# A four-layer graph stack on one core: layer 0 reads a turned copy of x, the gate's column rows come from v, and the first loads and all lists are set anew

## The reference

```python
# layer 0: 8 heads of 32, masked attention, layer norm
q, k, v = (proj(Wq, bq), proj(Wk, bk), proj(Wv, bv))
scores = jnp.where(mask, q @ k^T / sqrt(32), -inf)
x = layernorm(x + softmax(scores) @ v @ Wo.T + bo) * gamma + beta
# layer 1: 8 heads, gate a + c, log of the adjacency
a = x @ w_g[:D]
c = x @ w_g[D:]
scores = scores + (a[:, :, None] + c[:, None, :] + b_g + log(adjacency + EPS))
x = softmax(scores) @ V + x
# layer 2: graph attention, one head
logits = q + jnp.swapaxes(k, 2, 1); masked = logits + (1 - adj) * NEG_BIG
x = softmax(leaky(masked)) @ feat_proj + x
# layer 3: as layer 0, with log(clip(adj)) added to the scores
```

## Time and profile before

| | |
|---|---|
| median of 3 runs | 1913.1 us (1909.35 to 1915.19) |
| the profiled execution | 1908.63 us, span 1906.8 us |
| PE, DVE busy | 92%, 81% of the span |
| ACT, POOL busy | 64%, 65% of the span |
| transfers | 66.44 MB, 35 GB/s on average |

### The profile page before, as it was taken

How to read it: one execution, slowest core, us unless ns; L and a number is a source line. 1 busy time by engine, 2 the same in 40 slices (tenths; PEclk the granted TensorE clock), 3 DMA queues, 4 the chain that set the end, 5 groups by cost and what they waited for, 6 DMA issues and landing times.

```text
span 1906.8 us, 54647 instructions
## 1 busy us (share of the span) xinstructions
PE 1745.8 (92%) x23564; PEld 1334.6 (70%) x23564; DVE 1550.6 (81%) x2976; ACT 1216.3 (64%) x1894; POOL 1230.1 (65%) x743
## 2 busy tenths in 40 slices
PE   3899998899999999889999989888999999988996
PEld 2667776677777777577777767667777677766774
DVE  2889887777799988777889988777788998877775
ACT  1567665467777775456877767546777776654675
POOL 2534588368874377728895348754888445883688
PEclk9999999999999999999999999999999999999999
DMA  5110000100221001000111000010021100001001
GB/s 138 40 40 18 13 18 29 41 19 29 63 68 35 13 18 35 17 29 24 51 57 62 24 19 13 30 45 7 19 74 57 51 19 13 18 29 40 13 18 46
DMA packets 67731, 66.44 MB, mean 35 GB/s; under 512 B 6050, under 2 KB 67492, under 8 KB 67492
## 3 DMA queue, kind: packets, MB, share of 16 engines
q1 hardware_dynamic: 67492, 62.95, 11.1%
HBM read 54.54 MB, written 8.39 MB: 33 GB/s over the span
## 4 chain that ended last, share of the span: by engine, by line
PE 74%; DVE 19%; ACT 2%; issue 2%; SPq 1%; POOL 1%; DMA 0%; DVEq 0%; POOLq 0%; ACTq 0%
PE gx L589 22%; PE sc L694 16%; PE od L727 16%; PE gx L740 5%; PE gx L614 3%; PE sc L688 3%; DVE ring L969 3%; PE sc L700 3%; PE gx L776 3%; DVE negm L941 2%; DVE negm L944 2%; DVE qk L923 2%; PE gx L707 2%; DVE lg L1013 1%; DVE negm L957 1%
## 5 line engine op out<-in xcount | busy, mean ns | idle before, releaser
L574 POOL TENSOR_TENSOR ring<-ring,adj_c 128x1024 f32<-128x1024 f32 x256 | 610.4, 2409 | 170.0 <-ACT ring L837 113.0
L694 PE MATMUL sc<-qk 32*128 32x256 f32 x9216 | 417.4, 297 | 11.2 <-ACT m_rows L827 4.4
L694 PEld LDWEIGHTS sc<-qk 32*128 32x128 f32 x9216 | 326.0, 187 | 110.1 <-issue 64.3
L824 ACT ACTIVATE aside<-sc 128x1024 f32<-128x1024 f32 x192 | 196.6, 1024 | 236.1 <-PE sc L694 156.3
L941 DVE TENSOR_REDUCE negm<-sc 128x4 f32<-128x1024 f32 x192 | 234.1, 1219 | 86.2 <-PE sc L694 51.8
L839 ACT ACTIVATE ring<-sc 128x1024 f32<-128x1024 f32 x256 | 248.4, 1023 | 29.8 <-PE sc L700 29.3
L727 PE MATMUL od<-ring,vf 128*32 128x256 f32 x3072 | 243.4, 388 | 3.2 <-POOL ring L574 3.2
L553 POOL TENSOR_TENSOR xs<-xs,bo 128x512 f32<-128x512 f32 x96 | 128.0, 1333 | 182.0 <-DVE xt_lo L915 169.4
L727 PE MATMUL od<-ring,ones_r 128*32 128x256 f32 x3072 | 236.1, 379 | 0.0
L944 DVE TENSOR_REDUCE negm<-aside 128x4 f32<-128x1024 f32 x192 | 232.3, 1210 | 0.0
L579 POOL TENSOR_TENSOR xs<-xs,lr_g 128x512 f32<-128x512 f32 x64 | 86.9, 1357 | 169.8 <-ACT xs L846 169.8
(11 more groups left out here) (141 smaller groups left out, 4320.5 us busy)
## 6 DMA issues: line engine op xcount, KB each, us to landing
adj_c<-in_adj_t SPq DMA_DIRECT2D x96, 256.0 KB, 2.8
adj_r<-in_adj SPq DMA_DIRECT2D x64, 256.0 KB, 2.9
xs<-in_x SPq DMA_DIRECT2D x32, 256.0 KB, 3.1
out<-xs SPq DMA_DIRECT2D x32, 256.0 KB, 2.2
wo<-in_w_o SPq DMA_DIRECT2D x2, 256.0 KB
ring<-in_w_q SPq DMA_DIRECT2D x2, 256.0 KB, 6.5
ring<-in_w_k SPq DMA_DIRECT2D x2, 256.0 KB, 6.7
lr_g<-in_w_bg SPq DMA_DIRECT2D x2, 128.0 KB
```

Of the source, the lines that this page charges most:

```text
L574: pool.tensor_tensor(part, part, adj_c[i.mi % 3][:, t, :].unsqueeze(1).to_broadcast([P, G, N]), ALU.mult).then_inc(weighted, 1)
L694: mm = pe.matmul(sc[:, g, t * N:(t + 1) * N], buf[rows, a, c, t * P:(t + 1) * P], buf[rows, b, c, :], start=(n == 0 and not masked), stop= ...
L824: act.activation(aside[:], sc[:, 0:2, :], ACT.Copy).then_inc(set_aside, 1)
```

## The change

- **x of layer 0.** The host passes a turned copy `x_t` as well. A new stage LT on SP loads it into two buffers `x_raw`. In layer 0 T is only ACT's copy to `xt_hi` and DVE's `xt_lo`, both from `x_raw`; the four PE transposes are gone. LT waits until the `xt_lo` of the item two before is done, ACT's T until the projections that read the buffer are.
- **Gate's c.** `cr_hi`, `cr_lo`, `row_sel` and the six matmuls are gone. A new stage O takes column D + 1 of `vf`: two small DVE operations put its hi and lo into `c_pad`, two 128x128 matmuls turn it into `gx`, ACT copies it to `c_rows`.
- **First loads.** x_t of item 0 is SP's first load. ACT issues the weights q, k, v of layer 0 and their two bias columns on its own queue. The operands of `fold_biases` come next, the other small ones (`plain`) and the weights of layers 1 to 3 behind x of item 1. `extend_fc` now also waits for `w_plain`. POOL's scaling of q1 and q3 moves to PC of item 1.
- **Lists.** All tables have new numbers (GAT_START 24 to 25 and LAST_START 33.5 to 37.5 leave the order of the items as it is).

The diff, cut to its core (of the tables only some lines; of the functions the lines spoken of here):

```diff
-    "T": {PE: [-1.369], ACTE: [-0.812], DVE: [-0.531]},
-    "A": {PE: [13.457, 13.547, 15.008, 15.85]},
+    "T": {ACTE: [-1.791], DVE: [-1.732]},
+    "A": {PE: [13.511, 14.151, 14.428, 15.543]},
-    "U": {DVE: [7.002]},
-    "H": {DVE: [19.026]},
+    "O": {PE: [3.901], ACTE: [3.712], DVE: [2.701]},
+    "U": {DVE: [7.447]},
+    "H": {DVE: [18.738]},
+    "LT": {SP: [-10.005]},
...
+            sp.dma_start(x_raw[0][:], x_t_all[items_l0[0].batch]).then_inc(xt_loaded[0], 16)
+            sp.dma_start(adj_r[0][:], adj_all[rows_of[0].batch]).then_inc(adjr_loaded[0], 16)
+            for dst, src in fold_plain:
+                sp.dma_start(dst, src).then_inc(w_fold, 16)
+            sp.dma_start(x_raw[1][:], x_t_all[items_l0[1].batch]).then_inc(xt_loaded[1], 16)
             for s, i, c in order[SP]:
-                if s == "LX":
+                if s == "LT" and i.i0 >= 2:
+                    sp.wait_ge(xt_lo_set, items_l0[i.i0 - 2].k + 1)
+                    sp.dma_start(x_raw[i.i0 % 2][:], x_t_all[i.batch]).then_inc(xt_loaded[i.i0 % 2], 16)
+                elif s == "LX":
                     if i.k == GROUP - 1:
                         sp.wait_ge(w_lo_set, len(WEIGHTS))
                     if i.group:
                         sp.wait_ge(stored[i.slot], 16 * i.group)
                     sp.dma_start(xs[:, i.slot], x_all[i.batch]).then_inc(x_loaded[i.slot], 16)
-                    if i.k == 0:
-                        for dst, src in first_plain:
-                            sp.dma_start(dst, src).then_inc(w_first, 16)
-                        for n in range(3):
+                    if i.k == 1:
+                        for dst, src in plain:
+                            sp.dma_start(dst, src).then_inc(w_plain, 16)
+                        for n in range(3, len(WEIGHTS)):
                             load_weight(n)
                 elif s == "LR":
...
-                        pool.wait_ge(w_plain, 16 * len(plain))
-                    pool.wait_ge(xt_lo_set, i.k + 1)
+                    if i.l == 0:
+                        pool.wait_ge(*x_ready(i))
+                    else:
+                        pool.wait_ge(xt_lo_set, i.k + 1)
...
                 elif s == "PC":
+                    if i.k == 1:
+                        pool.wait_ge(w_plain, 16 * len(plain))
+                        for name in ("q1", "q3"):
+                            pool.tensor_scalar(b_col[name][:], b_col[name][:], SCALE, None, ALU.mult).then_inc(cols_set, 1)
...
-                pe.wait_ge(w_plain, 16 * len(plain))
+                pe.wait_ge(w_fold, 16 * len(fold_plain))
...
-                    if s == "P" and i.l == 1:
-
-                        if newcomer:
-                            pe.wait_ge(cw_set, CW_STEPS)
-                        pe.wait_ge(*gx_emptied("ca", i))
-                        project(gx_of("ca", i)[:, 0:N], [lambda h: cr_hi[:, h, :], lambda h: cr_lo[:, h, :]],
-                                [lambda h: xh[:, h, :], lambda h: xl[:, h, :]]).then_inc(gx_sem("ca", i), 1)
...
+                elif s == "O":
+
+                    pe.wait_ge(c_pad_set, i.i1 + 1)
+                    pe.wait_ge(*gx_emptied("ca", i))
+                    for n in range(T):
+                        mm = pe.matmul(gx_of("ca", i)[:, n * P:(n + 1) * P], c_pad[i.i1 % 2][:, n, :], ident_r[:], start=True, stop=True)
+                    mm.then_inc(gx_sem("ca", i), 1)
...
+            for n in range(3):
+                if n == 1:
+                    for dst, src in first_plain:
+                        act.dma_start(dst, src).then_inc(w_first, 16)
+                name = WEIGHTS[n]
+                act.dma_start(staged[name][:, :, 0:D], w[name].rearrange("(c p) e -> p c e", p=P)).then_inc(w_raw[n], 16)
             split(0)
             for s, i, c in order[ACTE]:
                 newcomer = i.group == 0 and i.slot == 0
                 if s == "I":
                     split(c)
                 elif s == "T":
-                    act.wait_ge(gx_sem("x", i), gx_count("x", i))
-                    act.activation(xt_hi[i.k % 2][:].rearrange("p c n -> p (c n)"), gx_of("x", i)[:], ACT.Copy)\
-                        .then_inc(xt_hi_set, 1)
+                    hi = xt_hi[i.k % 2][:].rearrange("p c n -> p (c n)")
+                    if i.l == 0:
+                        act.wait_ge(xt_loaded[i.i0 % 2], 16 * (i.i0 // 2 + 1))
+                        if i.k >= 2:
+
+                            j = items[i.k - 2]
+                            what = "fp1" if j.l == GAT else "vb" if j.l == 1 else "v"
+                            act.wait_ge(gx_sem(what, j), gx_count(what, j))
+                        act.activation(hi, x_raw[i.i0 % 2][:].rearrange("p c n -> p (c n)"), ACT.Copy).then_inc(xt_hi_set, 1)
+                    else:
+                        act.wait_ge(gx_sem("x", i), gx_count("x", i))
+                        act.activation(hi, gx_of("x", i)[:], ACT.Copy).then_inc(xt_hi_set, 1)
...
-                    if s == "P" and i.l == 1:
-                        act.wait_ge(gx_sem("ca", i), gx_count("ca", i))
-                        act.activation(c_rows[i.i1 % 2][:], gx_of("ca", i)[:, 0:N], ACT.Copy).then_inc(c_hi_set, 1)
...
+                elif s == "O":
+                    act.wait_ge(gx_sem("ca", i), gx_count("ca", i))
+                    act.activation(c_rows[i.i1 % 2][:], gx_of("ca", i)[:, 0:N], ACT.Copy).then_inc(c_set, 1)
...
+                dve.wait_ge(w_plain, 16 * len(plain))
...
-                    dve.tensor_tensor(xt_lo[i.k % 2][:].rearrange("p c n -> p (c n)"), gx_of("x", i)[:],
+                    turned_x = x_raw[i.i0 % 2][:].rearrange("p c n -> p (c n)") if i.l == 0 else gx_of("x", i)[:]
+                    dve.tensor_tensor(xt_lo[i.k % 2][:].rearrange("p c n -> p (c n)"), turned_x,
...
                                                  op0=ALU.add, op1=ALU.subtract).then_inc(qk_lo_set, 1)
-                    if s == "P" and i.l == 1:
-                        dve.wait_ge(c_hi_set, i.i1 + 1)
-                        rows = c_rows[i.i1 % 2]
-                        dve.scalar_tensor_tensor(out=rows[:], in0=rows[:].bitcast(F32), scalar=row_sel[:],
-                                                 in1=gx_of("ca", i)[:, 0:N], op0=ALU.mult, op1=ALU.add).then_inc(c_lo_set, 1)
...
+                elif s == "O":
+                    gate_c = vf[i.mi % NVF][:, :, D + 1:D + 2].to_broadcast([P, T, G])
+                    pad = c_pad[i.i1 % 2][:].rearrange("p t (g r) -> p t g r", g=G)
+                    dve.wait_ge(v_set, v_count(i))
+                    if i.i1 >= 2:
+                        dve.wait_ge(c_set, i.i1 - 1)
+                    dve.tensor_copy(pad[:, :, :, 0], gate_c).then_inc(c_hi_set, 1)
+                    dve.wait_ge(c_hi_set, i.i1 + 1)
+                    dve.tensor_tensor(pad[:, :, :, 1], gate_c, pad[:, :, :, 0].bitcast(F32), ALU.subtract).then_inc(c_pad_set, 1)
```

207 lines of the change are left out of this document (91 added, 116 removed).

## The result

| | time, us |
|---|---|
| before, median of 4 runs | 1911.9 (1909.35 to 1915.19) |
| after, median of 4 runs | 2080.8 (2077.0 to 2083.6) |
| ratio | 1.088, 95% interval 1.085 to 1.091 |
| profiled execution, before and after | spans 1906.8 and 2076.6 |

A forecast was written before the change was run, and what follows sets the result against it. The prediction took TensorE as the bound (busy 1745.8 of 1906.8 us), with PE waiting for others in layer 1. Start, layer 0 and layer 1's lock: 1908.6 - 20 - 4 + 24 + 8 = 1916.6, as a median 1921; range 1862 to 1946.

The forecast's parts named there:

- The start: Before the first Q: Q starts at about 7 us, W_fc's extension at 27; -20 us, bounds -25 and -12.
- rival D: First loads queue up behind each other, so the start gains only 12 us; 1929 us, chance 0.08.
- Layer 0: Its 32 items: removed turning matmuls save 0.53 us each, mostly lost again; -4 us, bounds -16 and +5.
- the gap: Layer 0 on PE: S, now directly behind P, waits for E's exps, 0.44 us plus 0.05 for the semaphore.
- Layer 1, own work: PE in layer 1: six matmuls on c leave, two for O come; -0.5 us an item, bound -16 for 32.
- Layer 1, DVE against POOL: POOL's ring multiply holds up U on DVE: items take 17.9 us instead of 15.3; +24, and +8 for Z items.
- rival C: PE's clock halves after idle stretches, 1.7 us each, four more per group, +27; 1948 us, chance 0.12.
- step (c): Layer 1 on DVE: H comes before U, so U starts 0.60 us later.
- The multiply: Layer 1 on POOL: E.1's ring multiply does not move; XB and PC fit into 3.48 us of POOL idle time.
- the norm's items: Layer 1, fourth and fifth item of a run, with Z: 1 us each for 8 items, +8.
- the first three: First three layer 1 items of each run, mixed with layer 0: 0, from -1.5 to +3 for all three.
- The rest: GAT: 0; layer 3: 0, bound +2.7 an item on the 20 without Z if the lock comes there.

The follow-up runs named there:

- h0: Kernel before with only the new first loads (x of item 0 first, not turned), all tables old: 1897.6 us, ratio 0.989.
- f2: Changed kernel with all its new tables, but stage O removed and c made by six matmuls behind P as before: one run, 2129.5 us.
- f4: Kernel before with one number changed: in layer 1 U stands behind H on DVE; one run, 2013.2 us.
- e2b: Changed kernel's code with the tables of the kernel before, except new layer 1 table and FIRST_PLAN left new: one run, 2099.9 us.
- experiments 1 and 2: Changed kernel's code, tables of the kernel before except FIRST_PLAN and O's own places: 2127.9 us; then the same with the new layer 1 table: 2099.9 us.
- h2: Kernel before with new first loads, U ahead of N on DVE in layer 1, POOL's Y behind E.0's multiply: 1880.8 us, ratio 0.980.
- g4: Changed kernel with POOL's layer 1 order and layer 0's Y (ACT, POOL) as before, U and O ahead of N and H on DVE: one run, 1935.9 us.

## Why the prediction was wrong

**The start: right in size but for its gate.** Q started at 7.0 as said. W_fc's extension started at 31.9 and not at 27, 15 us earlier than before and not 20. h0 gives the same: 25.1 us earlier and 9.3 lost again in layer 0, so some 16 where 20 was forecast with a bound of 12. The chain of waits:

```profile
15.35 10.27 DMA ring<-in_w_q
...
25.64 0.63 ACT wh_q L788
...
31.96 0.57 DVE ring L897
```

What was late was not W_fc but w_q of layer 1: issued at 15.35, it took 10.27 us to land, and its split stands in ACT's list ahead of work that item 1 needs. I had followed DVE's list to its load and not ACT's. The same load took 7.59 us in the kernel before, as SP's 25th; here it is the 30th and takes 10.27. That is what rival D spoke of: the loads did run into each other. That the Trainium skill, page "DMA: Bandwidth & Descriptors", section "Issuing engines are not separate DMA queues", says that such transfers share the same engines agrees with it.

**Layer 0: the gap came, and the bound was too small.** In the first group the first row below shows S's wait for the exps: 0.65, of which 0.23 is one of the four mask matmuls whose record is missing, so some 0.42 (forecast 0.44 and the semaphore). Items took 17.0 and not 17.4, in part since of three A's in a row the first two take 0.87 each, where single ones took 1.0. In the later groups the first three took 19.8 to 21.4 and the others 17.7 to 19.1. Timeline of PE in the first group, then of POOL, DVE and PE in a later one:

```profile
113.12 0.81 PE L681 MATMUL sc<-mask_r,ident_b 128*128 128x512 bf16 x3 [0.65 <-ACT ring L854]
...
603.43 2.15 POOL L581 TENSOR_TENSOR xs<-xs,lr_e 128x512 f32<-128x512 f32 x1
...
602.78 3.88 DVE L980 TENSOR_TENSOR ring<-ring,adj_c 128x1024 f32<-128x1024 f32 x2
...
612.77 1.29 POOL L549 TENSOR_TENSOR xs<-xs,bo 128x512 f32<-128x512 f32 x1
...
612.85 1.76 DVE L922 TENSOR_TENSOR xt_lo<-x_raw,xt_hi 128x512 fp32r<-128x512 f32 x1
...
611.87 0.62 PE L687 MATMUL sc<-qk 32*128 32x256 f32 x12 [1.67 <-DVE negm L943]
```

L980 takes 3.88 for two beside Y, so the reduction behind it on DVE (L943) ends late, and E, which needs the score buffer that it reads, waits 1.67. Behind that, L922 takes 1.76 beside XB. U is held more often in layer 0, too: in layer 0 of group 1 its two operations take 873 and 975 ns on average, where they took 466 and 516, and `xt_lo` 1395 instead of 680. That is 7 us more of DVE for U and 5 for `xt_lo`, in a group that became 13 us longer; which of it PE waited for is not set apart. The prediction had looked at U in layer 1 alone. It said of DVE that it would be full and of L922 that it could be held up, and left both at 0, with +5 for the whole as a bound. It was +47, the start's late gate included. A row of the groups of the kernel before would have given a bound (busy us, mean ns):

```profile
L969 DVE TENSOR_TENSOR ring<-ring,adj_c 128x1024 f32<-128x1024 f32 x128 | 181.6, 1459 | 0.3 <-issue 0.3
```

Half of these rows take no more than 1.22 us; the mean of 1459 says that even before, a sixth of their time was waiting for POOL.

**Layer 1, own work: not measured by itself.** Forecast were -0.5 us an item. f2 shows O worth 1.2 us an item against the six matmuls, but in lists where POOL holds DVE up, so that this holds more than the matmuls.

**Layer 1, DVE against POOL: the mechanism right, the size off by 4.** This is the step that failed. Forecast +32, measured +139, of which PE's idle time is +101 and most of the rest the clock. Three terms of the step were mis-sized:

- *The clock.* I had it as rival C at 1.7 for an idle stretch, one in five already there, and at 0 in the forecast. The step (c) alone costs 3.4 by the clock (f4: 8.76 against 5.32), and in the changed kernel the clock is at half for 10.24 us in each item, behind and through PE's two waits. The earlier trace rows had 0.98 because four of five items hardly idled; the mean hid what one idle stretch costs. It could be read there: the item behind the 2.69 us of idle in the earlier trace rows (Q at 731.50) took 16.8 us with PE busy all through at a clock of 0.90, and the one behind it 15.3 us. Five items a group at 3.4 would have made +68.
- *The multiply.* The prediction said that it does not move. It did. ACT's part of Y stands behind P now, so POOL's Y starts at 285.89, and E.0's multiply behind it ends at 293.2 instead of having ended before O. I had placed XB and PC into an idle time of 3.48 us that Y's delay had used up. So O, which I took to be free, was held for 2.3 us.
- *O on PE's path.* PE waits at O's matmuls between A.2 and A.3 (2.46), for O's operations and for H behind them. I had costed O's operations on DVE only and not asked who waits for them. Before, L930 read PSUM and was never held; its two successors read SBUF.

In group 1 the five items took 117.3 us where 89.5 and 2 for the norm's items were forecast; the first three, left at 0, took 60.0 instead of 58.3. **The rest**: layer 3 +3.4 a group, where the forecast had 0 (with POOL light 107 instead of 111, so POOL has a part in it), layer 2 -1.2.

The stretches add up, as they must: 1908.6 - 25.2 + 46.6 + 139.4 - 4.7 + 13.7 = 2078.4, the profiled execution of after.

What stays open: what decides whether an idle stretch brings the lower clock. 2.69 us of idle time did in the kernel before and 2.82 did not in e2b, so its price can't be told from its length alone; and which order frees DVE in layer 0.

## What to carry to other kernels

Where two engines can lock each other out, price a small operation not by its own time but by the longest instruction that can run beside it, for every place to which it moves, and look at what moves the other engine's instruction as well; one number in a table was worth 92 us here, and two numbers the other way, for U and Y, won 20 us in layer 1. A wait of a few microseconds on TensorE can cost more behind it, nothing in e2b's item and 3.4 us behind 4.4 in f4; read the clock of the stretch that follows a single idle time, not the mean of a window. When tables are mixed, list every one of them: one left new made experiments 1 and 2 say little about layer 0. And when a change mixes a sound part (the loads, 1%) with others, run the parts alone: the whole hid it.

## What the runs showed of the hardware

- TensorE's granted clock fell to half (1.2 GHz) behind many idle times of 2.5 to 5 us: for 3.4 us behind 2.69 of idle in the kernel before (0.50 in 732.34 to 735.75), and it was 0.52 over 8.76 us behind 4.4 of idle in f4. It did not fall behind all of them: it stayed at 1.00 behind 2.82 us in e2b (280.33 to 298.31) and behind 3.24 us in h2 (194.69 to 204.69). With idle times that come to at most 2.2 us an item it stayed at 1.00 (g4, 229 to 297 us).
- A DVE operation that reads only SBUF was held for up to a whole POOL instruction (2.3 us for 0.17 us of work), also by short ones: U's rows end with XB's and PC's. The Trainium skill, page "SBUF — State Buffer", section "SBUF: two separate sides", tells this as an exclusive lock for a whole instruction; with POOL light the means of O's and U's operations fell to a third or less and that of `xt_lo` to two thirds. Not every DVE operation on SBUF was held: in the changed kernel the reduction L946 of `aside`, the transpose L990 and the reciprocal L988 took 1.21, 0.45 and 0.20 us, whether POOL was at work or not.
- A 256 KB load took 4.12 us as the first of its queue (w_q of layer 0 in the changed kernel), 5.32 as the 37th of SP's queue in the kernel before, and 10.27 as the 30th in the changed one (w_q of layer 1, 7.59 before).
